# Pairs of heads: score halves alternate between two heads, one bias operation serves both, and the tile loop is written out

## The reference, cut to what matters

```python
x = x + attn(layernorm(x))        # q, k, v with rope; softmax over the 16 heads of one token
x = x + xattn(layernorm(x), ctx)  # the large part
x = x + moe(layernorm(x))         # 8 experts, top 2, and a shared one

# xattn: 16 heads of 16 numbers, 2048 queries, 2048 keys
q, k, v = fq_sym(q), fq_sym(k), fq_sym(v)        # rounded to 8 bits
attn = softmax(einsum('bhqd,bhkd->bhqk', q, k))
attn = fq_unsigned(attn)                         # clip(round(attn / (max/255)), 0, 255) * max/255
out  = einsum('bhqk,bhkd->bhqd', attn, v) @ Wp + bp
```

## Time and profile before

| what | us |
|---|---|
| median of 3 runs | 1199.38 (1195.58 to 1200.67) |
| the profiled execution | 1197.12 |
| its span in the trace | 1195.3 |
| DVE busy | 977.3 (82%) |
| PE busy | 945.0 (79%), mean granted clock 0.774 |
| POOL busy | 754.0 (63%) |
| ACT busy | 743.7 (62%) |
| DMA queue of the transposes | 69.8% of 16 engines |

### The profile page before, as it was taken

How to read it: one execution, slowest core, us unless ns; L and a number is a source line. 1 busy time by engine, 2 the same in 40 slices (tenths; PEclk the granted TensorE clock), 3 DMA queues, 4 the chain that set the end, 5 groups by cost and what they waited for, 6 DMA issues and landing times. The chain is left out here.

```text
span 1195.3 us, 25897 instructions
## 1 busy us (share of the span) xinstructions
PE 945.0 (79%) x8256; PEld 516.1 (43%) x8256; DVE 977.3 (82%) x1944; ACT 743.7 (62%) x971; POOL 754.0 (63%) x794
## 2 busy tenths in 40 slices
PE   6765678989896868888797978787787869788874
PEld 3434233544453434444444444444444434444443
DVE  5986979888897969888798879798797979788762
ACT  2443546666777665676667766666557677668562
POOL 6537787767767675777677667767677777711011
PEclk9876667768688877787786868887687979677687
DMA  6001577769787867697896977687687968679780
GB/s 206 1 36 40 99 135 132 127 118 168 125 151 116 147 117 123 127 132 136 126 168 116 152 115 140 117 146 127 114 147 124 168 121 152 121 136 144 132 146 10
DMA packets 541061, 148.24 MB, mean 124 GB/s; under 512 B 534130, under 2 KB 538868, under 8 KB 540532
## 3 DMA queue, kind: packets, MB, share of 16 engines
q1 hardware_dynamic: 540916, 146.44, 69.8%
HBM read 10.09 MB, written 2.10 MB: 10 GB/s over the span
## 5 line engine op out<-in xcount | busy, mean ns | idle before, releaser
L1071 DVE TENSOR_SCALAR_CACHE_REDUCE score<-ps_score,q_neg 128x1024 f32<-128x1024 f32 x512 | 640.8, 1279 | 110.1 <-PE ps_score L1423 95.2
L755 ACT ACTIVATE prob<-score,exp_bias 128x2048 uint8<-128x2048 f32 x256 | 512.4, 2002 | 148.9 <-DVE exp_bias L1081 148.5
L1423 PE MATMUL ps_score<-keys,queries 48*128 48x512 bf16 x1024 | 369.4, 457 | 105.6 <-DVE score L1071 93.2
L1445 PE MATMUL ps_pv<-prob_t,values 128*32 128x128 f16 x4096 | 213.8, 260 | 0.0
L547 POOL TENSOR_TENSOR product<-hs_exp,v_tok 128x1024 f32<-128x1024 f32 x64 | 183.0, 2860 | 36.8 <-ACT hs_exp L728 36.7
L553 POOL TENSOR_TENSOR folded<-product 128x512 f32<-128x512 f32 x128 | 163.2, 1275 | 43.6 <-POOL product L547 33.8
L1445 PEld LDWEIGHTS ps_pv<-prob_t,values 128*32 128x32 f16 x4096 | 182.8, 119 | 0.0
L1423 PEld LDWEIGHTS ps_score<-keys,queries 48*128 48x128 bf16 x1024 | 61.8, 99 | 256.2 <-DVE score L1071 186.7
L547 POOL TENSOR_TENSOR product<-qk_rot 128x1024 f32<-128x1024 f32 x64 | 150.7, 2355 | 2.6 <-issue 1.4
L1441 PE MATMUL ps_pv<-neg,values 128*32 128x128 f16 x1024 | 136.1, 259 | 11.5 <-DMA prob_t<-prob 11.3
L784 ACT ACTIVATE routed_both<-normed,routed_gate 128x256 bf16<-128x256 f32 x124 | 52.6, 496 | 89.6 <-POOL routed_gate L516 89.6
(11 more groups left out here) (136 smaller groups left out, 1276.8 us busy)
## 6 DMA issues: line engine op xcount, KB each, us to landing
prob_t<-prob SPq DMA_TRANSPOSE x256, 4.5
prob_t<-in_w SPq DMA_DIRECT2D x3, 1024.0 KB, 4.8
x_in<-in_x SPq DMA_DIRECT2D x16, 128.0 KB, 2.7
score<-in_cond_t SPq DMA_DIRECT2D x4, 512.0 KB, 7.1
out<-x_out SPq DMA_DIRECT2D x16, 128.0 KB, 2.4
w_qkv<-in_w_qkv SPq DMA_DIRECT2D x1, 768.0 KB, 4.1
early<-in_w_kv SPq DMA_DIRECT2D x1, 512.0 KB
w_s<-in_w_s SPq DMA_DIRECT2D x3, 128.0 KB
```

The source lines that it names most:

```text
L755: act.activation(prob[:, s, :].bitcast(U8)[:, 0::2], score[:, s, :], ACT.Exp, bias=exp_bias[:, s:s + 1], scale=-1.0, accum_out=prob_sum[:, ...
L1071: dve.tensor_scalar(score[:, s, HALF * i:HALF * i + HALF], ps_score[:, i].rearrange("p b k -> p (b k)"), q_neg[:, t.par, h:h + 1], None, A ...
L1423: mm = pe.matmul(ps_score[:, i, b, :], queries[lo:lo + 3 * HD, t.par, h // 2, :], keys[lo:lo + 3 * HD, h // 2, k0:k0 + KEYS], start=True, ...
L1445: mm = pe.matmul(out[j], beside_zeros(values, 4 * i + b, h + j), prob_t[:, (h + j) % RING, 4 * i + b, :], start=False, stop=(i == T // 4 - ...
```

## The change

Tiles are written out one after the other: the hardware loop is gone, `Tile` knows its number, and the registers with it.

In steps 2k and 2k + 1 the halves are dealt out anew. Before, step 2k did both halves of head 2k and step 2k + 1 both of head 2k + 1. Now step 2k does the first half of both heads (head 2k in slot 0, head 2k + 1 in slot 1) and step 2k + 1 the second half of both. The second half's operation starts from the first one's minimum (a second scalar operand, `low[:, s, 0:1]`), so that `low[:, s, 1]` is that of the whole row. The bias of both heads is then one `tensor_tensor` of 128x2, at the end of step 2k + 1. `exp_head(h)` waits for the count h // 2 + 1 of these. Nothing else is moved on any engine.

```diff
-def over_tiles(eng, body):
-    for t in range(3):
-        body(Tile(t, t, t % 2))
-    with eng.Fori(3, T - 4, 2) as t:
-        body(Tile(t, 3, 1))
-        body(Tile(t + 1, 4, 0))
-    for t in range(T - 3, T + 2):
-        body(Tile(t, t, t % 2))
+def over_tiles(body):
+    for t in range(T + 2):
+        body(Tile(t))
...
             def exp_head(h, t):
                 s = h % RING
-                act.wait_ge(bias_ready, t.count(H, h + 1))
+                act.wait_ge(bias_ready, t.count(H // 2, h // 2 + 1))
...
             def keep_scores(h, t):
-                s = h % RING
+                half = h % 2
                 for i in range(2):
+                    head = h - half + i
+                    s = head % RING
                     dve.wait_ge(score_made, t.count(2 * H, 2 * h + i + 1))
...
-                        if (due := t.due(H, h - RING + 1)) is not None:
+                    if half == 0:
+                        if (due := t.due(H, head - RING + 1)) is not None:
                             dve.wait_ge(prob_ready, due)
...
+                    else:
+                        dve.wait_ge(score_kept, t.count(2 * H, 2 * (h - 1) + i + 1))
-                    dve.tensor_scalar(score[:, s, HALF * i:HALF * i + HALF], ps_score[:, i].rearrange("p b k -> p (b k)"),
-                                      q_neg[:, t.par, h:h + 1], None, ALU.mult, ALU.min,
-                                      accum_out=low[:, s, i:i + 1]).then_inc(score_kept, 1)
+                    dve.tensor_scalar(score[:, s, HALF * half:HALF * half + HALF],
+                                      ps_score[:, i].rearrange("p b k -> p (b k)"), q_neg[:, t.par, head:head + 1],
+                                      low[:, s, 0:1] if half else None, ALU.mult, ALU.min,
+                                      accum_out=low[:, s, half:half + 1]).then_inc(score_kept, 1)

             def bias(h, t):
...
-                s = h % RING
-                dve.tensor_scalar(exp_bias[:, s:s + 1], low[:, s, 0:1], low[:, s, 1:2], LN255, ALU.min, ALU.add
-                                  ).then_inc(bias_ready, 1)
+                s = (h - 1) % RING
+                dve.tensor_tensor(exp_bias[:, s:s + 2], low[:, s:s + 2, 1], ln255[:], ALU.add).then_inc(bias_ready, 1)
...
-                    if t.exists():
+                    if t.exists() and h % 2 == 1:
                         bias(h, t)
...
             def scores(h, i, t):
-                lo = 64 * (h % 2)
+                half, lo = h % 2, 64 * i
...
-                    k0 = HALF * i + KEYS * b
+                    k0 = HALF * half + KEYS * b
```

More of the change, by code:

```diff
@@ L70, with __init__ @@
 class Tile:
-    def __init__(self, idx, least, par):
-        self.idx, self.least, self.par = idx, least, par
+    def __init__(self, idx):
+        self.idx, self.par = idx, idx % 2
     def __add__(self, n):
-        return Tile(self.idx + n, self.least + n, (self.par + n) % 2)
+        return Tile(self.idx + n)
     def starts(self):
-        return isinstance(self.idx, int) and self.idx == 0
+        return self.idx == 0
     def exists(self):
[L83 to L89, removed]
+        return 0 <= self.idx < T
     def count(self, n, extra=0):
@@ L403, in body @@
                         store(t + -2)
-            load_x(Tile(2, 2, 0))
+            load_x(Tile(2))
             sp.wait_ge(v_turned, T // 4)
-            over_tiles(sp, body)
+            over_tiles(body)
             sp.wait_ge(stored, 16 * T)
@@ L609, in body @@
                         value_products(h - 14, a)
-            first, second = Tile(0, 0, 0), Tile(1, 1, 1)
+            first, second = Tile(0), Tile(1)
             ln_scale(0, first)
@@ L887, in quantise_keys @@
                 dve.wait_ge(k_product, u + 1)
-                step = Tile(u, u, 0)
+                step = Tile(u)
                 dve.tensor_reduce(k_max[:], kp, AX.X, ALU.max, apply_absolute_value=True
@@ L1055, in keep_scores @@
             def keep_scores(h, t):
-                s = h % RING
+                half = h % 2
                 for i in range(2):
+                    head = h - half + i
+                    s = head % RING
                     dve.wait_ge(score_made, t.count(2 * H, 2 * h + i + 1))
[L1060 to L1066, removed]
-                        if (due := t.due(H, h - RING + 1)) is not None:
-                            dve.wait_ge(prob_ready, due)
-                        if h == 0:
-                            dve.wait_ge(q_chain, t.count(6, 6))
-                    dve.tensor_scalar(score[:, s, HALF * i:HALF * i + HALF], ps_score[:, i].rearrange("p b k -> p (b k)"),
-                                      q_neg[:, t.par, h:h + 1], None, ALU.mult, ALU.min,
-                                      accum_out=low[:, s, i:i + 1]).then_inc(score_kept, 1)
+                    if h == 0 and i == 0:
+                        dve.wait_ge(vt_product, T // 2)
+                        dve.wait_ge(k_product, T // 2)
+                        dve.wait_ge(q_chain, t.count(6, 6))
+                    if t.starts() and h == 2 and i == 1:
+                        dve.wait_ge(values_added, 4)
+                    if half == 0:
+                        if (due := t.due(H, head - RING + 1)) is not None:
+                            dve.wait_ge(prob_ready, due)
+                    else:
[4 more added lines that the diff above has]
+                                      accum_out=low[:, s, half:half + 1]).then_inc(score_kept, 1)
             def bias(h, t):
```

27 lines of the change are left out of this document (13 added, 14 removed).

## The result

The changed kernel takes 1393.99 us (median of 4 runs, 1391.81 to 1395.82) against 1198.58 us before: a ratio of 1.1632, 95% interval 1.1601 to 1.1663. That is 195 us more, where 54 more were forecast (1253 us, range 1205 to 1292). The sign was right, the size was not.

The account below looks back on a forecast made before the run. DVE's instructions in order, plus a few standstills per tile, were taken to bound the kernel. Loop -15, bias operations -10, second tanh +38 and items 2 to 5 +43 gave +56 on 1197.1 us: 1253 us, range 1205 to 1292.

Parts of the forecast that it names:

- items 2 to 5: Later exponentials delay `keep_ho` (step 7, 1.7 us), gate (10, 1.95), queries (12, 1.65), transposes (7, 0.5): +43 us net.
- the bias operations: On DVE, 128 of 256 go; those removed in steps 0, 4 and 6 save 0.64 us a tile: -10 us.
- The loop: At tile starts, four jumps back cost 3.8 us each, so writing the loop out gives -15 us.
- The second scalar operand: On DVE's second-half score operations: 0.02 us each, 256 of them +5 us at most; set to 0 with the new bias.
- The prediction's own sign of being wrong: One of three signs: DVE's second-half score operation visibly longer than 1.28 us.
- The second tanh: Item 1, step 1: the experts' tanh behind head 0's later exponential stalls DVE 2.7 us in 14 tiles, +38 us.
- The POOL wait: At step 13 DVE's 34.8 us of waits for POOL, with 8.8 us for `xq`, absorb 39 us of stalls.
- item 5: Step 7: later exponentials delay the transposes of heads 2 and 3 on PE, +0.5 us, +2.8 with the longest landing.
- Nothing is taken up: Rival, chance 0.17: `choose` passes its slack, POOL's chain moves with the stalls and transposes queue; +116 us, 1313 us.
- its 4.6 us: On POOL, slack between DVE's gate result (884.8) and `choose` (889.44); items 2, 3 and 5 use 3.9 us.
- Only the tanh counts: Rival, chance 0.18: waits for POOL and PE take up all of items 2 to 5; +13 us, 1210 us.
- faster: Rival, chance 0.12: ACT's late operations cost DVE nothing; jumps and bias operations give -25 us, 1172 us.

Follow-up runs that it names:

- pair_two_ops: The changed kernel with two old 128x1 bias operations in place of the 128x2 one: 1343.2 us.
- late_bias: The kernel before with its loop written out and both old biases of a head pair at the end of the odd step, halves as before: 1346.7 us.
- late_tanh: late_bias with the experts' second tanh one step earlier on ACT, ahead of head 0's exponential: 1307.4 us.
- unroll_only: The kernel before with only the tile loop written out; heads, biases and exponentials as before: 1187.4 us.
- pair_one_scalar: The changed kernel with the 128x2 bias as a tensor_scalar, one SBUF input and ln 255 as an immediate: 1392.7 us.
- pair_one_pointer: The changed kernel with the 128x2 bias as a tensor_scalar, one SBUF input and ln 255 as a scalar operand: 1399.1 us.
- probe_one_column: unroll_only plus one unread 128x1 DVE operation, SBUF to SBUF with an immediate, behind each odd step's bias: 1181.5 us.

## Why the prediction was wrong

From 1198.6 to 1394.0, by the kernels in a row: loop written out -13 (1187.4, with 1200.0 before in its job), delay +159 (1346.7), halves dealt out anew -4 (1343.2, not clear of noise), two-column bias +51 (1394.0). Two steps of the prediction failed: items 2 to 5, short by 77 us, and the bias operations, short by 61.

**The loop: right.** 15 us forecast, 13 measured, some 3 us for each of the four jumps. The 51 to 108 ns per branch that the Trainium skill gives (Advanced Engine Details and Errata, Control Flow Timing) would have made it under half a microsecond, an estimate from that page; the run disagrees with it as the price of this jump. What the engines wait for behind the jump isn't shown.

**The bias operations: a failed step.** The prediction took the new bias at 0.16 to 0.21 us from the nearest rows, with ends of 5 us either way, and the removed ones as 10 us gained. It measured 0.80 us on average and costs 51 us net, 61 from the -10 of the sum and far outside its ends. The wrong step is that a row of another form gives the price, as if an operation took the same time whatever POOL does. The rows are of a 128x1 bias and of one 128x8 operation that happened to start while POOL was idle. The same 128x8 group takes 0.287 us on average over the kernel before, a 128x16 one (`q_scale`) 0.398 with 0.17 in tile 11. I read one instance where the group's mean and maximum said that a few were held. The group, and one of its two long ones beside POOL's product, ending within 0.03 us of it:

```profile
L1114 DVE TENSOR_SCALAR gate<-gate_exp x16: 158/160/1326, 223.0 to 1174.1; 128x8 f32<-128x8 f32 x16
...
619.61 2.35 POOL L547 TENSOR_TENSOR product<-qk_rot 128x1024 f32<-128x1024 f32 x1
...
620.96 1.02 DVE L1114 TENSOR_SCALAR gate<-gate_exp 128x8 f32<-128x8 f32 x1
```

The second scalar operand was mis-sized too: 0.067 us in 256 operations, 17 us, where +5 was the most. The prediction's own sign of being wrong (a second half visibly longer than 1.28 us) did come. It cost nothing that shows in the time: pair_two_ops takes no longer than late_bias.

The Trainium skill (GPSIMD Engine Reference, Key points) says that VectorE and GpSimd share SBUF interfaces, with contention for VectorE instructions in a 2-port mode or with two SBUF inputs. The changed bias has two SBUF inputs, and the trace agrees in all 62 long ones. It was the rule that spoke against this change, and I passed over it for the one on branches. That the one-input forms of two columns are held as well agrees with it if they run in the 2-port mode, which no run here shows. What the kernel before shows is that, where neither is held (the first number), a one-input operation between SBUF and SBUF is faster than a two-input one of the same 128x512, 0.43 against 0.69 us:

```profile
L899 DVE TENSOR_SCALAR queries<-queries x8: 426/479/1870, 18.7 to 81.2; 128x512 f32<-128x512 f32 x8
...
L905 DVE TENSOR_TENSOR prob<-queries,k_scale x8: 693/912/3172, 20.3 to 81.7; 128x512 f32<-128x512 f32 x8
```

**The second tanh: right.** 38 forecast; DVE waits 40 us more there than before, and 39 us go when the tanh is moved away.

**Items 2 to 5: the other failed step, right places and about a third of the size.** Forecast +43 net; late_tanh against unroll_only gives 120. Each direct wait came in near or above its item: `x_one` 31 us (1.7 x 14 = 24), `gate` 27 more than in unroll_only (29), `q_max` 41 more (23), 99 together. The POOL wait that should take up 39 us took up 55. So the direct waits less the POOL wait come to 44, close to the forecast, partly by luck, since both are larger than their terms. What was missing is the step behind each: I let DVE stop where it needs the delayed result and then go on as today, a term that the prediction put at nothing without a reason. But `ho_project`, `gate_and_shared` and `xq` stand on PE ahead of the next scores, and in odd steps `times_values` stands in between. So DVE waits once for the result and again for the second score operation of the next step: with the 11 us at step 7, which belong to item 5, 70 us. The changed kernel's PE shows it around steps 8 to 11:

```profile
930.58 2.08 PE L1282 MATMUL ps<-w_o,ho_t 128*128 128x256 f32 x4 [3.38 <-ACT ho_t L717]
932.59 1.03 PE L1409 MATMUL ps_score<-keys,queries 48*128 48x512 bf16 x2
...
935.33 0.60 PE L1409 MATMUL ps_score<-keys,queries 48*128 48x512 bf16 x2
...
941.31 1.02 PE L1282 MATMUL ps<-w_gate,normed_t 128*128 128x8 f32 x4 [3.34 <-ACT normed_t L690]
942.19 1.20 PE L1282 MATMUL ps<-normed_t,w_s 128*128 128x128 f32 x4
943.32 1.03 PE L1409 MATMUL ps_score<-keys,queries 48*128 48x512 bf16 x2
...
946.53 1.03 PE L1409 MATMUL ps_score<-keys,queries 48*128 48x512 bf16 x2
```

PE stands idle for 3.38 us ahead of `ho_project`, which takes 2.08 us, 1.39 in the earlier trace rows; DVE waits 2.42 us for `x_one` (932.70) and again 0.77 us at 935.97. The second reason is the clock. The granted clock of these stretches (us, PE busy, granted clock, DMA share, GB/s), and behind them that of steps 7 to 12 of tile 11 before:

```profile
927.90:934.70 6.80, 4.12 (x28) 0.50 0.85 158
934.70:938.20 3.50, 2.73 (x30) 0.99 0.56 104
938.90:959.00 20.10, 14.29 (x98) 0.50 0.57 92
```

```profile
873.00:892.00 19.00, 17.75 (x166) 0.82 0.87 167
```

0.50 is the lower of its two levels (1.2 GHz against 2.4). It begins within the 3.38 us of idle time and stands through most of steps 8 to 12. There two score matmuls take 1.03 us against 0.60, and `xq` 3.2 us against 1.75 in the earlier trace rows. The lower level is not new: `xq` takes 3.2 us in 3 of the 16 tiles of unroll_only. But in late_bias it does so in 15 of 16, 1.1 us more on average. That is 18 us, and by as much `q_max` came in above its item. That the long waits bring the clock down isn't shown: in tile 11 before it is at the lower level too from 875.6 to 879.0, and no wait of PE in this stretch is longer than 0.60 us. The mean granted clock goes from 0.774 to 0.721 in late_bias and 0.698 in the changed kernel. How the 70 us of second waits divide between queue and clock wasn't separated.

**The rivals.** "Nothing is taken up" (1313 us) was the nearest in size, against the 1347 of late_bias, and it had 0.17. Half of its mechanism came: in late_bias POOL waits for the gate at the start of `choose` in all 16 tiles, 54.0 us, against 20.4 us in 3 tiles in unroll_only. So `choose` did pass its 4.6 us, which the prediction held free. But the wait for POOL was taken up all the same, and what makes the time longer is the second waits on PE, which that rival doesn't have. "Only the tanh counts" and "faster" fall with late_bias.

## What to carry to other kernels

When a producer starts later, list everything that stands behind it on its in-order engine, then what stands behind each of *those* on the next engine: a wait of PE inside its stream of score matmuls is paid at the result and again at the next scores. Moving the first late exponential behind its neighbours (three lines on ACT) gave back 122 of 159 us. And a tiny operation of DVE between SBUF and SBUF isn't priced by its size where GpSimd runs long ones: look up the group's mean and maximum, not an instance, and keep 128x1 forms if these aren't held.

## What the runs showed of the hardware

- A DVE operation of 128x2 from SBUF to SBUF, with two inputs, with an immediate or with a scalar operand, does not end before the POOL `tensor_tensor` of 128x1024 that runs when it starts: up to 2.1, 2.3 and 2.2 us instead of 0.11 to 0.18 (changed kernel, pair_one_scalar, pair_one_pointer), in all 62, 65 and 61 cases. The 128x1 forms were never held: 0.146 us at most in 128 (probe_one_column), 0.22 in the 256 old biases of pair_two_ops.
- It isn't only these forms: in the kernel before, 128x8, 128x16, 128x512 and 128x2048 operations from SBUF to SBUF are held as well, for up to some 2.5 us each.
- The hardware loop with its four jumps back and its register waits costs 12.6 us (1200.0 less 1187.4), 1.05% by these medians and 1.4% by the ratio over the rounds (0.6 to 2.1%).
- A reduction with a start value as second scalar operand takes 1.342 us instead of 1.275 over 1024 columns from PSUM, 0.067 us more.
